# Regrouping attention heads by direct transfers between on-chip buffers, slot by slot

## The chip, the cores and the metric

The kernel runs on one core of one Trainium2 chip. The metric is device time in microseconds. A core has TensorE (PE, matmuls), VectorE (DVE), ScalarE (ACT) and GpSimd (POOL), each with its own list of instructions run in order; SyncE (SP) issues most of the DMA transfers, also in order; sixteen DMA engines carry them. Engines meet through semaphores: an instruction waits until a counter has reached a number, and adds to a counter when it is done. A DMA adds 16.

## The reference

x has 4 x 1024 tokens of 256 numbers. The "attention" mixes heads within a token and never tokens with each other. Then come a layer norm, a mixture of experts (32 experts, 4 picked per token) with a shared expert, and another layer norm, all in float32:

```
Q, K, V = (x @ W.T).reshape(b, s, 16, 16)  for W in Wq, Wk, Wv
scores  = einsum('bshd,bstd->bsht', Q, K) / 4        # 16 x 16 for each token
out     = einsum('bsht,bstd->bshd', softmax(scores), V).reshape(b, s, 256)
x = layernorm(x + out @ Wfc.T)
x = layernorm(x + experts(x, top 4 of 32) + shared_expert(x))
```

## The kernel before

The 4096 tokens go in 8 chunks of 512. For each chunk TensorE projects Q, K and V (`project`, six parts of 128 rows each), with the 256 rows of a projection on 2 x 128 partitions and the 512 tokens along a row. ScalarE copies each part to the buffers `QT`, `KT`, `VT` (`evacuate`). A token's 16 x 16 scores need another layout: there the 512 tokens are cut into 8 slots of 64, partition 16 t + d holds dimension d of slot t, and a row holds 16 heads x 64 tokens. Then one matmul does a token from each slot at once; `Q2`, `K2` and `V2` have zeros wherever slots would mix. The same way back leads from `O_sb`, which has the outputs in the slot layout, to `OT`, which `out_project` reads.

The kernel before changes layout through memory. SP writes a tensor to `q_slots` and the like, one piece of 64 tokens (256 bytes) at a time, waits until it has landed, and reads it back in rows of 4 KB: `write_q`, `write_k`, `write_v`, `read_q`, `read_k`, `read_v` (lines 322 to 369). For O the write has 4 KB rows and the read 256-byte pieces: `write_o`, `read_o` (lines 371 to 381). Per chunk these are 2 + 2 transfers for Q, 2 + 8 for K, 4 + 4 for V and 1 + 2 for O.

There is one `Q2`, one `K2`, one `V2` and one `O_sb`: the next chunk's Q and K may be read in only when the last score matmul of the chunk before is done (`s_ready`), V only after its last weighing matmul (`o_ready`), and O is copied out by ScalarE in two halves (`copy_o`, `o_copied`) before it is written. `OT` exists twice.

All orders are written out by hand. TensorE's list mixes the projections of chunks ahead with scores, weighing and output projection of chunks behind (`score`, `weigh`, `out_project`, lines 1017 to 1046). VectorE does softmax, residual sums (`residual`, line 1447), variance and the routing of tokens to experts. GpSimd does one small step of the layer norm (line 575) and scatters the routed rows to memory, 16 scatters a chunk (line 582). SP's list runs from line 383 to line 502. When all 8 chunks are routed, the expert stage begins: SP loads rows of an expert, TensorE transposes and multiplies them, and the results are scattered, loaded and summed. The big expert weights lie in the memory that the attention buffers had, and are loaded when these are free (lines 482 to 502).

In rows and views one line can stand for many steps: line 1003 is the helper for all matmuls, 670 and 673 are the copies of Q, K and V, 682 that of O. `wgu_sb` holds Q2, K2, V2 and O_sb; `wd_sb` holds QT, KT, VT and OT; `sx` holds the normalised tokens.

Of the kernel before, what the change touches and what calls it, by code (L numbers as in the profile page):

```python
# [5 lines left out]
F32 = mybir.dt.float32  # L6
# [79 lines left out]
def build(nc, xT, x, wqkv, wfc, wr, rbias, wsgu, wsd, wgu, wd, out):  # L86
    xs = nc.dram_tensor("expert_rows", [XROWS, ROW], F32).ap()
    z = nc.dram_tensor("pick_rows", [TOPK * NTOK, DM], F32).ap()
    q_slots = nc.dram_tensor("q_slots", [CH, SLOT, DM, GRP], F32).ap()
    k_slots = nc.dram_tensor("k_slots", [CH, SLOT, DM, GRP], F32).ap()  # L90
    v_slots = nc.dram_tensor("v_slots", [CH, SLOT, DM, GRP], F32).ap()
    o_slots = nc.dram_tensor("o_slots", [CH, SLOT, DM, GRP], F32).ap()

    with ExitStack() as ctx:
# [164 lines left out]
        q_wr k_wr v_wr o_wr q_rd k_rd v_rd o_rd  # L259
# [18 lines left out]
        NSMALL = 5 * 16  # L278
        NCONST = 13
# [24 lines left out]
        def slot_rows(dram, n):  # L304
            return dram[n].rearrange("t r g -> r t g")

        @block.sync
        def _(sp):
# [23 lines left out]
            def write_k(n):
                write_slots(k_slots, KT, n, 4, S["k_wr"])

            def write_v(n):
                sp.wait_ge(S["evac"], 6 * n + 6)
                for hh in range(KC):
                    for t in range(2):
                        sp.dma_start(v_slots[n].rearrange("(c t) r g -> t r c g", t=2)[t, hh * P:(hh + 1) * P],
                                     VT[:, hh, t * 256:(t + 1) * 256].rearrange("p (c g) -> p c g", c=4))\  # L340
                            .then_inc(S["v_wr"], 16)

            def read_q(n):
                sp.wait_ge(S["q_wr"], 32 * (n + 1))
                if n:
                    sp.wait_ge(S["s_ready"], 2 * n)
                rows = q_slots[n].rearrange("t (d h) g -> (t d) (h g)", d=HD)
                for half in range(QB):
                    sp.dma_start(Q2[half * 64:(half + 1) * 64, half * 1024:(half + 1) * 1024],
                                 rows[half * 64:(half + 1) * 64, :]).then_inc(S["q_rd"], 16)  # L350

            def read_k(n, pairs):
                sp.wait_ge(S["k_wr"], 32 * (n + 1))
                if n:
                    sp.wait_ge(S["s_ready"], 2 * n)
                rows = k_slots[n].rearrange("t (d h) g -> (t d) (h g)", d=HD)
                for pair in pairs:
                    for t in range(2 * pair, 2 * pair + 2):
                        sp.dma_start(K2[t * HD:(t + 1) * HD, (t % KB) * 1024:(t % KB + 1) * 1024],  # L359
                                     rows[t * HD:(t + 1) * HD, :]).then_inc(S["k_rd"], 16)  # L360

            def read_v(n):
                sp.wait_ge(S["v_wr"], 64 * (n + 1))
                if n:
                    sp.wait_ge(S["o_ready"], 2 * n)
                rows = v_slots[n].rearrange("t (j d) g -> (t j) (d g)", d=HD)
                for c in range(KB):
                    sp.dma_start(V2[c * 32:(c + 1) * 32, c * 1024:(c + 1) * 1024],  # L368
                                 rows[c * 32:(c + 1) * 32, :]).then_inc(S["v_rd"], 16)
# [35 lines left out]
            write_q(2)
            read_k(1, range(0, 1))
            read_q(1)
            read_k(1, range(1, 2))
            write_k(2)
            read_k(1, range(2, 4))  # L410
            load_xT(4)
            write_v(2)
            read_v(1)
            write_o(0)
            write_q(3)
            read_o(0)
            read_q(2)
            read_k(2, range(0, 2))
            write_k(3)
            read_k(2, range(2, 4))  # L420
# [3 lines left out]
            read_v(2)
            write_o(1)
            write_q(4)
            read_k(3, range(0, 1))
            read_o(1)
            read_k(3, range(1, 2))
            read_q(3)  # L430
            read_k(3, range(2, 3))
            write_k(4)
            read_k(3, range(3, 4))
            read_v(3)
            write_o(2)
            read_o(2)
            load_x(3)
            read_k(4, range(0, 1))
            read_q(4)
            read_k(4, range(1, 2))  # L440
            write_v(4)
            read_k(4, range(2, 3))
# [3 lines left out]
            write_q(5)
            write_k(5)
            read_q(5)
            read_k(5, range(0, 1))
            read_v(4)  # L450
            write_o(3)
            read_k(5, range(1, 4))
            read_o(3)
# [3 lines left out]
            write_q(6)
            read_v(5)
            write_o(4)
            read_q(6)  # L460
# [1550 lines left out]
```

## Time and profile before

| | us |
|---|---|
| median of 3 runs (578.54 to 580.25) | 580.22 |
| the profiled execution as a whole | 585.22 |
| its span in the profile | 583.4 |

| stage of the span, us | TensorE busy | VectorE busy | DMA share | GB/s |
|---|---|---|---|---|
| 20 to 120 | 95.30 | 51.20 | 0.95 | 243 |
| 120 to 245 | 113.13 | 102.03 | 0.86 | 265 |
| 245 to 312 | 60.06 | 47.21 | 0.71 | 257 |

The first two stages are attention and routing, the third is the end of routing; from about 312 us on the experts run. The time from outside is longer than the span, and the profiled execution is longer than the median; sums are made within it. A row of a timeline gives start and length in microseconds, and in brackets for how long its engine stood idle before it and what ended that.

### The profile page before, as it was taken

Reading aid. Unit: us, or ns where it says so; the run is one execution under the profiler, and the core shown is the slowest. Engines: PE = TensorE matmul, PEld = TensorE weight load, DVE = VectorE, ACT = ScalarE, POOL = GpSimd, SP = SyncE. Lnnn points to the kernel's source line nnn. Section 1 sums busy time; section 2 is a strip of 40 time slices with the busy share of each in tenths; the row PEclk is TensorE's granted clock in tenths of the full one; section 3 lists DMA queues with packets and bytes.
Section 4 is the critical chain, followed back from the end, with each engine's and each line's share of the span. In section 5 each row is a group of like instructions: output and inputs, shape, how many; then the busy total and the mean of one; then the engine's idle time right before and its main releaser. Section 6 shows DMA issues by size and latency. Waiting matters only on the chain.

```text
span 583.4 us, 16223 instructions
## 1 busy us (share of the span) xinstructions
PE 532.9 (91%) x4604; PEld 402.9 (69%) x4605; DVE 353.0 (61%) x1207; ACT 296.2 (51%) x641; POOL 285.1 (49%) x293
## 2 busy tenths in 40 slices
PE   5989999997979999789888999999999999988994
PEld 2445667565647566556445999999988888877883
DVE  2032647897876899677943444444446666555865
ACT  1324463765646574423403566666655555545454
POOL 5000000664676767567770466666666655555400
PEclk9999999998989999899997999999999999999999
DMA  7998998997697999799623354555577777778398
GB/s 252 250 245 201 235 258 200 275 258 219 206 273 241 275 272 406 258 405 348 232 102 85 112 152 144 161 183 171 160 224 227 226 238 222 230 220 295 138 386 292
DMA packets 132219, 135.31 MB, mean 232 GB/s; under 512 B 77128, under 2 KB 115535, under 8 KB 131536
## 3 DMA queue, kind: packets, MB, share of 16 engines
q1 hardware_dynamic: 105984, 87.53, 52.6%
q0 software_dynamic: 12672, 34.10, 15.4%
q10 hardware_dynamic: 13520, 13.13, 7.5%
q8 instruction: 25, 0.41, 0.3%
q14 instruction: 18, 0.15, 0.1%
HBM read 74.79 MB, written 60.96 MB: 233 GB/s over the span
## 4 chain that ended last, share of the span: by engine, by line
PE 49%; DMA 18%; DVE 14%; SPq 6%; issue 6%; ACT 3%; DVEq 2%; ACTq 1%; POOL 1%; POOLq 0%
PE bank L1003 44%; DMA o_slots<-wgu_sb 5%; DMA prod<-expert_rows 5%; PE bank L1359 3%; DMA wd_sb<-o_slots 3%; DMA wgu_sb<-pick_rows 2%; SPq L368 1%; DVEq L299 1%; DMA pick_rows<-prod,ids 1%; ACT sx L972 1%; SPq L359 1%; DVE hsT L1527 1%; DMA wqkv_sb<-in_wqkv 1%; DVE hsT L1524 1%; SPq L522 1%
## 5 line engine op out<-in xcount | busy, mean ns | idle before, releaser
L616 POOL DMA_INDIRECT pick_rows<-prod,ids x134 | 139.2, 1039 | 101.8 <-ACT prod L929 75.8
L582 POOL DMA_INDIRECT expert_rows<-stage,pos x128 | 127.2, 994 | 58.9 <-issue 36.4
L1003 PE MATMUL bank<-prod 128*128 128x128 f32 x1088 | 134.8, 278 | 0.6 <-DVE prod L1845 0.6
L1003 PEld LDWEIGHTS bank<-prod 128*128 128x128 f32 x1088 | 129.0, 194 | 1.0 <-issue 0.9
L1003 PE MATMUL bank<-wd_sb,wqkv_sb 128*128 128x512 f32 x192 | 91.9, 615 | 6.3 <-DMA wqkv_sb<-in_wqkv 6.3
L1845 DVE COPY prod<-wgu_sb 128x512 f32 x136 | 54.0, 438 | 67.7 <-issue 59.3
L929 ACT ACTIVATE prod<-bank,kept 128x256 f32<-128x256 f32 x136 | 57.3, 470 | 31.3 <-PE bank L1003 27.7
L1003 PEld LDWEIGHTS bank<-wgu_sb 128*32 128x32 f32 x2048 | 58.8, 136 | 20.2 <-issue 17.0
L1003 PE MATMUL bank<-wgu_sb 128*32 128x64 f32 x2048 | 66.2, 296 | 4.6 <-DMA wgu_sb<-k_slots 3.7
L1003 PE MATMUL bank<-wd_sb,prod 128*128 x272 | 70.1, 380 | 0.4 <-DVE prod L1863 0.4
L1003 PEld LDWEIGHTS bank<-wd_sb,wqkv_sb 128*128 128x128 f32 x192 | 35.2, 195 | 42.5 <-issue 36.1
L575 POOL TENSOR_TENSOR rstdt<-vepst,neg_half 128x4 f32<-128x4 f32 x8 | 9.2, 1155 | 102.7 <-DVE vepst L1460 102.6
L1359 PE MATMUL bank<-ident,prod 128*128 128x128 f32 x272 | 43.0, 282 | 11.4 <-DMA prod<-expert_rows 7.8
L1359 PEld LDWEIGHTS bank<-ident,prod 128*128 128x128 f32 x272 | 32.5, 143 | 25.7 <-issue 10.6
L1003 PEld LDWEIGHTS bank<-wd_sb,prod 128*128 128x128 f32 x272 | 46.5, 191 | 4.3 <-issue 0.8
L1863 DVE TENSOR_TENSOR prod<-prod,bank 128x256 f32<-128x256 f32 x68 | 28.6, 420 | 34.3 <-ACT prod L945 33.5
L1003 PE MATMUL bank<-prod,wsgu_sb 128*128 128x512 f32 x96 | 45.2, 619 | 3.9 <-DVE hsT L1527 3.9
L1003 PE MATMUL bank<-wfc_sb,wd_sb 128*128 128x256 f32 x128 | 35.1, 423 | 11.5 <-DMA wd_sb<-o_slots 10.8
L920 ACT ACTIVATE prod<-bank 128x512 f32<-128x512 f32 x68 | 40.6, 597 | 1.5 <-PE bank L1359 1.5
L1003 PEld LDWEIGHTS bank<-wfc_sb,wd_sb 128*128 128x128 f32 x128 | 26.2, 211 | 21.8 <-issue 17.1
L661 ACT ACTIVATE stage<-sx 128x1024 f32<-128x1024 f32 x32 | 33.9, 1059 | 12.4 <-DVE idw L1612 5.5
L945 ACT ACTIVATE prod<-bank 128x256 f32<-128x256 f32 x68 | 26.0, 382 | 27.2 <-PE bank L1003 24.4
(170 smaller groups left out, 650.9 us busy)
## 6 DMA issues: line engine op xcount, KB each, us to landing
prod<-expert_rows SPq DMA_DIRECT2D x136, 132.0 KB
wsgu_sb<-pick_rows ACTq DMA_DIRECT2D x32, 256.0 KB, 3.8
wgu_sb<-pick_rows SPq DMA_DIRECT2D x12, 512.0 KB, 10.7
wgu_sb<-in_wgu SPq DMA_DIRECT2D x2, 2560.0 KB, 13.1
expert_rows<-pad_rows SPq DMA_DIRECT2D x4, 1056.0 KB, 19.1
wd_sb<-in_xT SPq DMA_DIRECT2D x8, 512.0 KB, 5.0
q_slots<-wd_sb SPq DMA_DIRECT2D x16, 256.0 KB
k_slots<-wd_sb SPq DMA_DIRECT2D x16, 256.0 KB, 4.2
```

Of the source, the lines that this page charges most:

```text
L299: return eng.value_load(tab[0:1, bass.ds(quad + SLOTS, 1)], min_val=0, max_val=NE ** (QUAD + 2) - 1)
L575: pool.tensor_tensor(rstdt[:, :], vepst[:, :], neg_half[:, :], ALU.pow).then_inc(S["rstd_ready"], 1)
L582: pool.indirect_dma_start(xs, bass.IndirectOffsetOnAxis(ap=pos[e % 2][:, i, k:k + 1], axis=0), stage[:, i, k, :], None, bounds_check=XROWS ...
L616: pool.indirect_dma_start(z, bass.IndirectOffsetOnAxis(ap=index[:, j:j + 1], axis=0), rows[:, j, :], None, bounds_check=TOPK * NTOK - 1, o ...
L661: act.activation(stage[:, i, :, 0:DM], x1_of(e)[:, i, :].unsqueeze(1).broadcast_to([P, TOPK, DM]), ACT.Copy)
L920: act.activation(xtT[par][:, :], banks[2][:, :], ACT.Copy).then_inc(S["cX_copied"], 1)
L929: act.activation(to[:, j, :], banks[6 + par][:, j * DM:(j + 1) * DM], ACT.Copy, scale=kept[par][:, j, 1:2]).then_inc(S["cy_copied"], 1)
L945: act.activation(cth[par][:, :], banks[par][:, 0:2 * P], ACT.Silu)\
L1003: return pe.matmul(dst, lhsT, rhs, start=(k == 0), stop=(k == n - 1))
L1359: last = pe.transpose(banks[2][:, c:c + P], xt[par][:, j, k * P:(k + 1) * P], ident[:, :])
L1845: last = dve.tensor_copy(ws[par][:, j, :], wgu_sb[:, bass.ds(found[j], KC * 2 * EI)])
L1863: dve.tensor_tensor(hT[par][:, :], cth[par][:, :], banks[par][:, 2 * P:4 * P], ALU.mult)\
```

## The change

The four tensors in memory go, and with them every write and read. In their place stand `regroup_q`, `regroup_k`, `regroup_v` and `regroup_o`: for each of the 8 slots one transfer of 64 KB from buffer to buffer, between 128 partitions x 2 x 64 numbers on one side and 16 partitions x 16 x 64 on the other. So that the order of numbers agrees on both sides, the columns of the weights are permuted on the host. The transfers of a tensor count on one semaphore: `q_in`, `k_in`, `v_in`, `o_in`, 8 x 16 a chunk.

`QT`, `KT` and `VT` now exist twice: odd chunks use room in `sx` that the last three chunks' normalised tokens need later, and the last chunk's V uses a buffer of x. ScalarE therefore waits for the transfers of two chunks before when it copies, and for those of the last chunks in `normalise`. TensorE's instructions and their order are unchanged, only the semaphores they wait for. SP's list is written anew.

```
+        def qT_of(n):
+            return over(sx, (CH - 1) * TPC * DM, KC, CT) if n % 2 else QT
...
-            def write_slots(dram, tensor, n, done, landed):
-                sp.wait_ge(S["evac"], 6 * n + done)
-                for hh in range(KC):
-                    sp.dma_start(slot_rows(dram, n)[hh * P:(hh + 1) * P],
-                                 tensor[:, hh, :].rearrange("p (t g) -> p t g", t=SLOT))\
-                        .then_inc(landed, 16)
...
+            def regroup_q(n):
+                sp.wait_ge(S["evac"], 6 * n + 2)
+                if n:
+                    sp.wait_ge(S["s_ready"], 2 * n)
+                for t in range(SLOT):
+                    sp.dma_start(Q2[t * HD:(t + 1) * HD, (t // 4) * 1024:(t // 4 + 1) * 1024],
+                                 qT_of(n)[:, :, slot(t)]).then_inc(S["q_in"], 16)
...
+            def regroup_o(n):
                 sp.wait_ge(S["o_copied"], 2 * (n + 1))
...
+                for t in range(SLOT):
+                    sp.dma_start(OT[n % 2][:, :, slot(t)], O_sb[t * NH:(t + 1) * NH, :]).then_inc(S["o_in"], 16)
...
+            regroup_o(1)
+            regroup_v(2)
...
-                if a and j % 2 == 0:
-                    act.wait_ge(S[("q_wr", "k_wr", "v_wr")[j // 2]], (64 if j == 4 else 32) * a)
+                if a >= 2 and j % 2 == 0:
+                    act.wait_ge(S[("q_in", "k_in", "v_in")[j // 2]], IN * (a - 1))
...
                 if p:
-                    act.wait_ge(S["o_wr"], 16 * p)
+                    act.wait_ge(S["o_in"], IN * p)
...
+                if b >= CH - 3:
+                    act.wait_ge(S[("v_in", "k_in", "q_in")[b - (CH - 3)]], IN * (CH - 2 if b == CH - 3 else CH))
...
-                pe.wait_ge(S["q_rd"], 32 * (p + 1))
-                pe.wait_ge(S["k_rd"], 128 * (p + 1))
+                pe.wait_ge(S["q_in"], IN * (p + 1))
+                pe.wait_ge(S["k_in"], IN * (p + 1))
```

On SP, around the V of chunk 2, the kernel before has this piece of its list (L339 writes V, L368 reads it, L373 writes O, L318 loads x):

```order
L339 DMA v_slots<-wd_sb 128x4x64 [waits evac]
L339 DMA v_slots<-wd_sb 128x4x64 x3
L318 DMA prod<-in_x 128x4x256 [waits res_ready]
L368 DMA wgu_sb<-v_slots 32x1024 [waits o_ready,v_wr]
L368 DMA wgu_sb<-v_slots 32x1024 x3
L373 DMA o_slots<-wgu_sb 128x1024 [waits o_copied]
```

The kernel after has there the following (L335 is Q, L343 K, L359 O, L351 V, L317 the load of the transposed x):

```order
L335 DMA wgu_sb<-wd_sb 16x16x64 [waits s_ready,evac]
L335 DMA wgu_sb<-wd_sb 16x16x64 x7
L343 DMA wgu_sb<-wd_sb 16x16x64 [waits s_ready,evac]
L343 DMA wgu_sb<-wd_sb 16x16x64 x7
L317 DMA wd_sb<-in_xT 128x1024 [waits proj_ready]
L359 DMA wd_sb<-wgu_sb 128x2x64 [waits o_copied]
L359 DMA wd_sb<-wgu_sb 128x2x64 x7
L351 DMA wgu_sb<-wd_sb 16x16x64 [waits o_ready,evac]
L351 DMA wgu_sb<-wd_sb 16x16x64 x7
```

The O of chunk 1 stood behind the V of chunk 2 and now stands ahead of it.

On SP, from the Q of chunk 5 to the O of chunk 3, the kernel before has (L349 and L359 read Q and K, L373 and L380 write and read O):

```order
L349 DMA wgu_sb<-q_slots 64x1024 [waits s_ready,q_wr]
L349 DMA wgu_sb<-q_slots 64x1024
L359 DMA wgu_sb<-k_slots 16x1024 [waits s_ready,k_wr]
L359 DMA wgu_sb<-k_slots 16x1024
L368 DMA wgu_sb<-v_slots 32x1024 [waits o_ready,v_wr]
L368 DMA wgu_sb<-v_slots 32x1024 x3
L373 DMA o_slots<-wgu_sb 128x1024 [waits o_copied]
L359 DMA wgu_sb<-k_slots 16x1024 [waits s_ready,k_wr]
L359 DMA wgu_sb<-k_slots 16x1024 x5
L380 DMA wd_sb<-o_slots 128x8x64 [waits y_ready,o_wr]
L380 DMA wd_sb<-o_slots 128x8x64
```

and the kernel after (`sx` is the odd chunk's buffer):

```order
L335 DMA wgu_sb<-sx 16x16x64 [waits s_ready,evac]
L335 DMA wgu_sb<-sx 16x16x64 x7
L343 DMA wgu_sb<-sx 16x16x64 [waits s_ready,evac]
L343 DMA wgu_sb<-sx 16x16x64 x7
L359 DMA wd_sb<-wgu_sb 128x2x64 [waits y_ready,o_copied]
L359 DMA wd_sb<-wgu_sb 128x2x64 x7
```

All of K now goes ahead of O, and V of chunk 4, which stood between Q and O, has moved behind O.

## Rows read from the trace of the kernel before

**Rows 1.** The page's first line.

```profile
span 583.4 us, 16223 instructions
```

**Rows 2.** List of waits, TensorE for regrouping: total us, times, longest.

```profile
PE bank L1003 <- DMA wd_sb<-o_slots: 10.8, 5, 4.0
...
PE bank L1003 <- DMA wgu_sb<-k_slots: 3.7, 2, 2.6
```

**Rows 3.** TensorE's timeline: scores, weighing (wgu_sb) and output projection (wfc_sb).

```profile
35.64 2.21 PE L1003 MATMUL bank<-wgu_sb 128*32 128x64 f32 x64 [2.62 <-DMA wgu_sb<-k_slots]
...
65.44 1.97 PE L1003 MATMUL bank<-wfc_sb,wd_sb 128*128 128x256 f32 x8 [0.76 <-DMA wd_sb<-o_slots]
...
86.99 1.98 PE L1003 MATMUL bank<-wgu_sb 128*32 128x64 f32 x64
...
135.67 2.21 PE L1003 MATMUL bank<-wgu_sb 128*32 128x64 f32 x64 [1.07 <-DMA wgu_sb<-k_slots]
139.81 3.15 PE L1003 MATMUL bank<-wfc_sb,wd_sb 128*128 128x256 f32 x8 [1.94 <-DMA wd_sb<-o_slots]
...
167.69 3.65 PE L1003 MATMUL bank<-wfc_sb,wd_sb 128*128 128x256 f32 x8 [3.96 <-DMA wd_sb<-o_slots]
...
182.81 2.21 PE L1003 MATMUL bank<-wgu_sb 128*32 128x64 f32 x64
...
243.45 3.34 PE L1003 MATMUL bank<-wfc_sb,wd_sb 128*128 128x256 f32 x8 [3.40 <-DMA wd_sb<-o_slots]
```

**Rows 4.** Busy us by engine, granted clock, DMA share, GB/s, output matmuls at 167.69.

```profile
core 0: us, PE busy (x) PEld busy (x) DVE busy (x) ACT busy (x) POOL busy (x), PEclk, DMA share, GB/s
...
167.69:171.34 3.65, 3.65 (x9) 2.96 (x10) 0.91 (x5) 0.00 (x0) 2.74 (x4) 0.53 0.86 248
```

**Rows 5.** VectorE's timeline: its waits for TensorE.

```profile
143.10 0.70 DVE L1447 TENSOR_TENSOR prod<-prod,bank 128x512 f32<-128x512 f32 x1 [2.89 <-PE bank L1003]
...
171.48 0.69 DVE L1447 TENSOR_TENSOR prod<-prod,bank 128x512 f32<-128x512 f32 x1 [2.77 <-PE bank L1003]
...
185.09 0.69 DVE L1478 TENSOR_REDUCE smax<-bank 128x32 f32<-128x512 f32 x1 [3.69 <-PE bank L1003]
...
246.93 0.69 DVE L1447 TENSOR_TENSOR prod<-prod,bank 128x512 f32<-128x512 f32 x1 [0.70 <-PE bank L1003]
...
252.09 0.69 DVE L1447 TENSOR_TENSOR prod<-prod,bank 128x512 f32<-128x512 f32 x1 [1.99 <-PE bank L1003]
```

**Rows 6.** Two stretches: only 256-byte pieces in flight; the early stage.

```profile
30.20:31.20 1.00, 1.00 (x4) 0.43 (x3) 0.00 (x0) 0.03 (x1) 0.00 (x0) 1.00 1.26 285
...
20.00:120.00 100.00, 95.30 (x1202) 60.26 (x1204) 51.20 (x140) 48.48 (x84) 13.22 (x13) 1.00 0.95 243
```

**Rows 7.** Line 325, 12 to 40 us: ns to issue (min/median/max), landing.

```profile
L325 SPq DMA_DIRECT2D q_slots<-wd_sb x6: 386/508/584, 12.9 to 39.2; - x6
L325 SPq DMA_DIRECT2D k_slots<-wd_sb x4: 360/502/584, 16.5 to 31.5; - x4
...
DMA to landing us min/median/max: 2.3/2.7/3.1
```

**Rows 8.** SP's timeline: start, us for the transfers merged into one row.

```profile
12.89 1.01 SPq L325 DMA_DIRECT2D q_slots<-wd_sb  x2
...
46.31 4.27 SPq L359 DMA_DIRECT2D wgu_sb<-k_slots  x4
...
123.37 1.09 SPq L349 DMA_DIRECT2D wgu_sb<-q_slots  x2
...
195.97 3.59 SPq L359 DMA_DIRECT2D wgu_sb<-k_slots  x8
```

**Rows 9.** ScalarE's timeline: second halves of O copied, chunks 1, 4 and 7.

```profile
77.23 0.99 ACT L682 ACTIVATE wgu_sb<-bank 128x512 f32<-128x512 f32 x1
...
155.05 1.03 ACT L682 ACTIVATE wgu_sb<-bank 128x512 f32<-128x512 f32 x1
...
231.53 1.04 ACT L682 ACTIVATE wgu_sb<-bank 128x512 f32<-128x512 f32 x1
```

**Rows 10.** Line 349, reads of Q from memory: landing.

```profile
DMA to landing us min/median/max: 3.5/4.4/7.1
```

**Rows 11.** GpSimd's timeline: the layer norm step of chunk 7.

```profile
254.66 1.04 POOL L575 TENSOR_TENSOR rstdt<-vepst,neg_half 128x4 f32<-128x4 f32 x1 [2.68 <-DVE vepst L1460]
```

More of the change, by code:

```diff
@@ L173, in x1_of, with kT_of, vT_of @@
             return over(sx, b * TPC * DM, TPC, DM)
+        def qT_of(n):
+            return over(sx, (CH - 1) * TPC * DM, KC, CT) if n % 2 else QT
+        def kT_of(n):
+            return over(sx, (CH - 2) * TPC * DM, KC, CT) if n % 2 else KT
+        def vT_of(n):
+            if n == CH - 1:
+                return xT_sb[0]
+            return over(sx, (CH - 3) * TPC * DM, KC, CT) if n % 2 else VT
         stage = sb("stage", [P, TPC, TOPK, ROW])
@@ L332, in write_k @@
[L332 to L341, printed above, removed]
@@ L343, in read_q, with slot @@
-            def read_q(n):
-                sp.wait_ge(S["q_wr"], 32 * (n + 1))
+            def slot(n):
+                return slice(n * GRP, (n + 1) * GRP)
+            def regroup_q(n):
+                sp.wait_ge(S["evac"], 6 * n + 2)
                 if n:
                     sp.wait_ge(S["s_ready"], 2 * n)
[L347 to L350, printed above, removed]
@@ L352, in read_k, with regroup_k @@
-            def read_k(n, pairs):
-                sp.wait_ge(S["k_wr"], 32 * (n + 1))
+                for t in range(SLOT):
+                    sp.dma_start(Q2[t * HD:(t + 1) * HD, (t // 4) * 1024:(t // 4 + 1) * 1024],
+                                 qT_of(n)[:, :, slot(t)]).then_inc(S["q_in"], 16)
+            def regroup_k(n):
+                sp.wait_ge(S["evac"], 6 * n + 4)
                 if n:
                     sp.wait_ge(S["s_ready"], 2 * n)
[L356 to L360, printed above, removed]
@@ L362, in read_v, with regroup_v @@
-            def read_v(n):
-                sp.wait_ge(S["v_wr"], 64 * (n + 1))
+                for t in range(SLOT):
+                    sp.dma_start(K2[t * HD:(t + 1) * HD, (t % KB) * 1024:(t % KB + 1) * 1024],
+                                 kT_of(n)[:, :, slot(t)]).then_inc(S["k_in"], 16)
+            def regroup_v(n):
+                sp.wait_ge(S["evac"], 6 * n + 6)
                 if n:
                     sp.wait_ge(S["o_ready"], 2 * n)
[L366 to L369, printed above, removed]
@@ L371, in write_o @@
-            def write_o(n):
+                for t in range(SLOT):
+                    sp.dma_start(V2[t * NH:(t + 1) * NH, (t // 2) * 1024:(t // 2 + 1) * 1024],
+                                 vT_of(n)[:, :, slot((t % 2) * 4 + t // 2)]).then_inc(S["v_in"], 16)
+            def regroup_o(n):
                 sp.wait_ge(S["o_copied"], 2 * (n + 1))
-                sp.dma_start(o_slots[n].rearrange("t (h d) g -> (t h) (d g)", d=HD), O_sb).then_inc(S["o_wr"], 16)
-            def read_o(n):
-                sp.wait_ge(S["o_wr"], 16 * (n + 1))
@@ L405, in _ @@
[L405 to L410, printed above, removed]
-            load_xT(4)
[L412 to L420, printed above, removed]
+            load_xT(3)
+            regroup_q(1)
+            regroup_k(1)
@@ L421, in _ @@
+            regroup_o(0)
+            regroup_v(1)
+            load_xT(4)
+            regroup_q(2)
+            regroup_k(2)
             load_xT(5)
-            write_v(3)
+            regroup_o(1)
+            regroup_v(2)
             load_x(2)
[L424 to L436, printed above, removed]
-            load_x(3)
[L438 to L442, printed above, removed]
+            regroup_q(3)
+            regroup_k(3)
+            regroup_o(2)
+            load_x(3)
+            regroup_v(3)
+            regroup_q(4)
+            regroup_k(4)
             load_xT(6)
-            read_k(4, range(3, 4))
@@ L445, in _ @@
             load_x(4)
[L446 to L453, printed above, removed]
+            regroup_q(5)
+            regroup_k(5)
+            regroup_o(3)
+            regroup_v(4)
             load_xT(7)
-            write_v(5)
             load_x(5)
[L457 to L460, printed above, removed]
@@ L485, in _ @@
             sp.dma_start(wgu_sb[:, 0:width], wgu[:, 0:width]).then_inc(S["big_w"], 16)
-            write_o(7)
-            read_o(7)
+            for landed in ("q_in", "k_in", "v_in"):
+                sp.wait_ge(S[landed], IN * CH)
+            sp.dma_start(wd_sb[:, 0:WD_EARLY * DM], wd[:, 0:WD_EARLY * DM]).then_inc(S["big_w"], 16)
+            regroup_o(7)
             sp.wait_ge(S["o_ready"], 2 * CH)
-            sp.wait_ge(S["o_rd"], 32 * CH)
+            sp.wait_ge(S["o_in"], IN * CH)
             half = (GU_EARLY + 10) * KC * 2 * EI
```

80 lines of the change are left out of this document (29 added, 51 removed).

## The prediction

> **What bounds the kernel now.** I read the page first: one execution of 583.4 us span [rows 1]. Then, on the engine with the most work, the list of waits: all that TensorE waits for the regrouping of Q, K, V and O through memory is 10.8 us on O and 3.7 us on K [rows 2]. Then TensorE's timeline: in the attention stage (up to about 250 us) its instructions stand almost end to end, and the regrouping shows as gaps of 2.62 us at 35.64, 0.76 at 65.44, 1.07 at 135.67, 1.94 at 139.81, 3.96 at 167.69 and 3.40 at 243.45 [rows 3]. A gap costs more than its length: the eight output matmuls take 1.97 us at 65.44, but 3.15, 3.65 and 3.34 us behind the three long gaps [rows 3]; in the longest the granted clock was 0.53 of full [rows 4], nearly all at the lower level (1.2 GHz), after TensorE had stood idle. That is another 1.2, 1.7 and 1.4 us. In all 13.8 us of gaps and 4.3 of clock.
>
> But TensorE is not alone. VectorE's timeline from 113 us on is one run of work after another, each started by a wait for TensorE: 2.89 us before 143.10, 2.77 before 171.48, 3.69 before 185.09, 0.70 before 246.93, 1.99 before 252.09 [rows 5]. A lead that TensorE wins is passed on only until the gap on VectorE is closed. These gaps sum to 12.0 us. GpSimd, which writes the routed rows, waits 2.68 us at 254.66 for chunk 7's variance [rows 11] and from there works through; so the expert stage starts earlier by as much as that instruction does. Expert stage and tail hold none of the changed transfers: I leave them as they are.
>
> **The change part by part.** I call lead the time by which an instruction runs ahead of the kernel before.
>
> *DMA volume.* Each chunk's four tensors of 512 KB were written to memory and read back; now they move once. The 256-byte pieces remain, 2048 to a tensor. While such pieces alone were in flight they moved at 285 GB/s [rows 6], so 512 KB need 1.84 us of all engines. In the early stage the DMA engines were 0.95 busy at 243 GB/s [rows 6]; half the traffic of this kind goes. So DMA time is no longer the limit, if pieces from buffer to buffer cost what pieces to memory do (rival 1).
>
> *SP's issues.* 25 regrouping transfers a chunk become 32. The nearest shape, 128x8x64, is issued in 508 ns at the median, 360 at least [rows 7]; two of them stand in 1.01 us [rows 8]. With the gap to the next instruction I take p = 0.55 us, so 8p = 4.4 us for a tensor. Below, 0.40 (the 360 plus the gap); above, 1.07, the four K reads that took 4.27 us at 46.31, where SP was held back, as I read it, by a full queue [rows 8]. I take the value near the median, since the queue should be emptier: a tensor is issued in 4.4 us and moves in 1.84. A chunk now costs SP 32 x 0.55 plus two loads, 18.7 us, and TensorE's first five chunks follow each other at (135.67 - 35.64)/5 = 20.0 us [rows 3]. SP fits in, barely.
>
> *Tail.* From the last issue to landing I take 2.3 us, the least of the 256 KB stores while little else ran (median 2.7) [rows 7]; upper end 4.4, the median of the Q reads from memory [rows 10]; lower end 1.5, an estimate: 2.3 less the 0.9 that the 256 KB themselves need at 285 GB/s.
>
> *Chunk 0.* Q goes at 12.89 as before [rows 8], K behind it, landed 12.9 + 8.8 + 2.3 = 24.0; TensorE arrives at 35.64 - 2.62 = 33.0. Gap gone: lead 2.6. O(0) lands well before 62, so 0.76 goes too: lead 3.4.
>
> *A new wait: V(2).* SP runs in order, and O(1) now stands ahead of V(2). O(1) waits for its copy, which ended at 77.23 + 0.99 = 78.2 [rows 9], now 74.8; O(1) is issued to 79.2, V(2) to 83.6, landed 85.9. TensorE wants V(2) at 86.99 - 3.4 = 83.6 [rows 3]. Late by 2.3: lead 1.1. Behind it SP has next to no slack through chunks 3 and 4 (18.7 against 20.0).
>
> *Chunk 5 and O(3).* SP's issue of Q(5) started at 123.37 on the score before it [rows 8], now 122.2. Q(5) and K(5) are issued to 131.0, landed 133.3; TensorE is there at 135.67 - 1.07 - 1.1 = 133.5. The 1.07 goes: lead 2.2. O(3) follows, issued to 135.4, landed 137.7, against 139.81: lead 2.1, so most of that gap stays, as a wait behind two tensors of issues and no longer as a round trip. VectorE's start at 143.10 gains the same 2.1.
>
> *O(4).* Its copy ended at 155.05 + 1.03 [rows 9], now 154.0; issued to 158.4, landed 160.7. TensorE is there at 167.69 - 3.96 - 2.1 = 161.6. Gap and slow clock go. VectorE then has no gap before 171.48: lead 2.1 + 2.77 = 4.9. The score of chunk 6 stood 15.1 us behind these output matmuls (182.81 - 167.69), 13.4 without the slow clock: it starts at 175.0 and takes 2.21, so VectorE's start of 185.09 becomes 177.3: lead 7.8, which the rest up to O(7) keeps.
>
> *O(7).* Copied at 231.53 + 1.04 [rows 9], now 224.8; issued to 229.2, landed 231.5; the large weight loads ahead of it move by the same lead. TensorE wants it at 243.45 - 3.40 - 7.8 = 232.2. Gap and clock go; VectorE gains its 0.70 and 1.99: lead 10.5 at 252.09, and GpSimd's 254.66 follows, its work before being 7.8 ahead and its gap 2.68, just enough.
>
> *At nothing.* ScalarE's new waits before it overwrites Q, K and V buffers are for transfers two chunks back; those before the last three normalisations are for transfers that land tens of microseconds earlier by the above. Weights' columns are reordered on the host.
>
> Sum: 583.4 - 10.5 = 572.9 of span [rows 1]; the profiled execution as a whole took 585.22, so 574.7; it lies 5.0 above the median of the runs, 580.22, which becomes 569.7.
>
> **Rivals.**
>
> *1. Transfers into 16 partitions drain more slowly than they are issued.* For it: the 1.07 us apiece at 46.31 were such transfers [rows 8]. Against: eight of them went in 3.59 us at 195.97, 0.45 apiece [rows 8]. With p = 0.62 (the most in rows 7, 584 ns, with the gap) a tensor takes 5.0 us: Q(2), K(2) and V(2) come by the same walk 4.6 us late in all, K(4) 1.7, K(5) 1.0, so the lead at chunk 5 is about -3; then O(4), the score of chunk 6 and O(7) give their 8 back: lead 5, 575 us.
> The Trainium skill (SBUF — State Buffer, "Door 1: The DMA port swizzle") speaks for this: a transfer's rate depends on how many of 16 ports its partitions reach, and partitions 0 to 15 reach four, measured at 104 GB/s. By that rule 64 KB need about 0.63 us, an estimate from that figure; the row at 195.97 took in 64 KB each 0.45 us, 146 GB/s, which is above it, but shows acceptance and not landing. By the one the sum is 575, by the other 569.7.
>
> *2. The tail is as long as through memory.* With 4.4 us for 2.3, V(2) is late by 4.4, K(4) and K(5) by some 2, O(3) lands at 144.9; the late stages give back 7: lead 2, 578 us, hardly to be told from no change. For it: no landing among them is under 2.3 [rows 7, 10]. Against: those move 256 KB, these 64.
>
> *3. SP becomes the engine that bounds.* Nothing of this shape was ever issued here: a side of 128 partitions against one of 16. At p = 0.75 a chunk costs SP 25.1 us against the 20.0 of TensorE; four chunks lose 5.1 each, 20 us, and the 2.6 of the start and about 7 of the late gaps are all that returns: 591 us. It decides from p = (20.0 - 1.1)/32 = 0.59 on, and at 3.2 x 4 = 13 us per 0.1 us it eats the gain of 10.5 at about p = 0.67. For it: 1.07 in the full queue. Against: the median of 0.51 for a larger transfer of three dimensions.
>
> **How the numbers follow.** Forecast 0.50, its own range 563 to 574 (p from 0.40 to 0.60); rival 1 0.18; rival 2 0.12; rival 3 0.15; 0.05 for more than forecast (all 18 us of gap and clock, about 562). A measurement of this kernel can tell 0.3%, 1.7 us. Faster: forecast, rival 1, the small rest, and a quarter of rival 2, 0.75; same 0.10; slower 0.15. The range runs from 562 to 585, leaving out most of rival 3.
>
> **What would show it.** Right: SP's issues near 0.5 us, eight in 4 to 4.5 us; no gap on TensorE at the first score, none at O(4) and O(7), the output matmuls there back at 2 us; a new gap of about 2 us at the weighing of chunk 2, and some 2 us left at O(3); DMA share clearly under 0.9 in the first 120 us; the first expert transposes some 10 us earlier. Wrong: issues of 0.65 us or more, or gaps on TensorE for Q and K at chunks 2 to 5; then SP bounds. If the gaps go and the end does not come earlier, VectorE or GpSimd has taken them.

## The result and the profile after

The changed kernel takes 596.98 us (median of 4 runs, 594.18 to 598.8) against 580.24 us before (4 runs, 578.54 to 581.45): 1.0287 times as long, with a 95% interval of 1.0234 to 1.0339. The prediction was 569.7. The profiled execution of after was the fastest of its four, that of before (585.22) slower than all four of its runs, so the two traces differ by 9.0 us of span only [rows 1]; what is read from them are places, not the total.

The page of after: span, SP's DMA queue (packets, MB, share of 16 engines), the chain that ended last by engine.

```profile
span 592.4 us, 16265 instructions
...
q1 hardware_dynamic: 102784, 70.76, 41.5%
...
PE 47%; SPq 14%; DMA 13%; issue 9%; POOL 5%; ACT 4%; DVE 4%; DVEq 1%; ACTq 1%; POOLq 1%
```

The queue moves 16.8 MB less than before (87.53 MB); SP's share of the chain, SPq, is 14% where it was 6%.

TensorE's waits for the regrouping, against [rows 2] (total us, times, longest):

```profile
PE bank L937 <- DMA wgu_sb<-wd_sb: 10.6, 2, 5.7
...
PE bank L937 <- DMA wd_sb<-wgu_sb: 8.7, 3, 4.9
...
PE bank L937 <- DMA wgu_sb<-sx: 6.7, 3, 3.0
```

The waits for O (`wd_sb<-wgu_sb`) have fallen a little, from 10.8 to 8.7 us; those for Q and K (from `wd_sb` in even chunks, from `sx` in odd ones) have risen from 3.7 to 17.3. TensorE's timeline shows where, against [rows 3]:

```profile
32.95 2.21 PE L937 MATMUL bank<-wgu_sb 128*32 128x64 f32 x64
...
61.92 1.89 PE L937 MATMUL bank<-wfc_sb,wd_sb 128*128 128x256 f32 x8
...
77.95 2.21 PE L937 MATMUL bank<-wgu_sb 128*32 128x64 f32 x64 [4.99 <-DMA wgu_sb<-wd_sb]
...
102.13 2.21 PE L937 MATMUL bank<-wgu_sb 128*32 128x64 f32 x64 [1.50 <-DMA wgu_sb<-sx]
...
126.69 7.76 PE L937 MATMUL bank<-wgu_sb 128*32 128x64 f32 x256 [5.66 <-DMA wgu_sb<-wd_sb]
...
145.57 2.21 PE L937 MATMUL bank<-wgu_sb 128*32 128x64 f32 x64 [2.14 <-DMA wgu_sb<-sx]
152.67 3.63 PE L937 MATMUL bank<-wfc_sb,wd_sb 128*128 128x256 f32 x8 [4.89 <-DMA wd_sb<-wgu_sb]
...
180.07 3.58 PE L937 MATMUL bank<-wfc_sb,wd_sb 128*128 128x256 f32 x8 [3.01 <-DMA wd_sb<-wgu_sb]
...
220.52 2.21 PE L937 MATMUL bank<-wgu_sb 128*32 128x64 f32 x64 [3.03 <-DMA wgu_sb<-sx]
...
255.77 1.97 PE L937 MATMUL bank<-wfc_sb,wd_sb 128*128 128x256 f32 x8 [0.78 <-DMA wd_sb<-wgu_sb]
...
324.25 0.66 PE L1293 MATMUL bank<-ident,prod 128*128 128x128 f32 x4 [2.51 <-DMA prod<-expert_rows]
```

The last row is the first transpose of the expert stage. In the kernel before it stands at:

```profile
311.82 0.66 PE L1359 MATMUL bank<-ident,prod 128*128 128x128 f32 x4
```

The first scores start 2.7 us earlier (32.95 for 35.64). Then the scores of chunks 2, 3, 4 and 5 each wait, and the lead turns into a lag: 9.9 us at chunk 5 (145.57 for 135.67), 12.9 at O(3) (152.67 for 139.81). From there it stays: 12.4 at O(4), 12.3 at O(7), 12.4 at the first expert transpose (324.25 for 311.82). From there to the end of the span the kernel after takes 3.4 us less in these two executions, which makes the 9.0. The output matmuls behind the long gaps at O(3) and O(4) run at 3.6 us instead of 2. So the loss arises between 52 and 153 us. What does SP do there? Its timeline over one whole chunk of issues (L335 is Q, L343 K, L359 O, L351 V, L317 and L323 load x), against [rows 8]:

```profile
64.83 5.20 SPq L335 DMA_DIRECT2D wgu_sb<-wd_sb  x8
70.13 5.98 SPq L343 DMA_DIRECT2D wgu_sb<-wd_sb  x8
76.16 0.60 SPq L317 DMA_DIRECT2D wd_sb<-in_xT  x1
76.80 6.07 SPq L359 DMA_DIRECT2D wd_sb<-wgu_sb  x8
82.97 5.23 SPq L351 DMA_DIRECT2D wgu_sb<-wd_sb  x8
88.24 0.61 SPq L323 DMA_DIRECT2D prod<-in_x  x1
88.95 5.21 SPq L335 DMA_DIRECT2D wgu_sb<-sx  x8
```

Each row starts within 0.1 us of the end of the one above: SP issues almost without a pause, and one round (Q, K, O, V and two loads, 64.83 to 88.95) takes 24.1 us where TensorE took 20.0 a chunk before. The issue times of line 335 (ns, min/median/max), against [rows 7], and the early stage as a whole, against [rows 6]:

```profile
L335 SPq DMA_DIRECT2D wgu_sb<-wd_sb x32: 566/617/1488, 12.6 to 172.0; - x32
L335 SPq DMA_DIRECT2D wgu_sb<-sx x32: 565/618/1847, 39.3 to 211.4; - x32
```

```profile
20.00:120.00 100.00, 91.91 (x1108) 57.80 (x1107) 46.84 (x132) 44.71 (x76) 10.11 (x10) 0.97 0.53 130
```

An issue takes 0.617 us at the median and now and then 1.1 to 1.9 us; with the 0.04 to the next, eight take 5.2 us, and 5.7 to 6.5 when one of them is slow. The DMA engines meanwhile are busy to 0.53, at 130 GB/s, where they were at 0.95 and 243. The chain of waits from 60 to 130 us puts the two together:

```profile
by line: PE bank L937 28.2%; SPq L343 22.5%; SPq L335 19.9%; DMA wgu_sb<-wd_sb 7.1%; SPq L351 5.5%; issue 5.3%; DMA wgu_sb<-sx 3.3%; ACT sx L630 3.0%; ACT stage L593 1.3%; SPq L317 0.9%; ACT wd_sb L602 0.9%; PE bank L985 0.8%; ACT sx L602 0
...
75.49 2.32 DMA wgu_sb<-wd_sb
```

Nearly half of that stretch is SP issuing Q, K and V (22.5, 19.9 and 5.5%). The last issue of K(2) lands 2.32 us later, and TensorE starts.

### The profile page after: what moved, and what is told of

It reads as the page before. It is cut to its first block, busy times and chain, and to the rows that moved or that the text cites. A ratio compares the mean times of both kernels' runs of the same rounds, so it can differ in the third digit from the quotient of the medians.

```text
span 592.4 us, 16265 instructions
## 1 busy us (share of the span) xinstructions
PE 528.0 (89%) x4604; PEld 400.6 (68%) x4605; DVE 353.2 (60%) x1207; ACT 296.1 (50%) x641; POOL 286.4 (48%) x293
## 3 DMA queue, kind: packets, MB, share of 16 engines
q1 hardware_dynamic: 102784, 70.76, 41.5%
q0 software_dynamic: 12672, 34.10, 15.5%
## 4 chain that ended last, share of the span: by engine, by line
PE 47%; SPq 14%; DMA 13%; issue 9%; POOL 5%; ACT 4%; DVE 4%; DVEq 1%; ACTq 1%; POOLq 1%
PE bank L937 42%; SPq L335 4%; SPq L343 4%; PE bank L1293 4%; DMA pick_rows<-prod,ids 4%; DMA prod<-expert_rows 4%; POOL expert_rows L514 3%; SPq L359 3%; DMA wgu_sb<-pick_rows 2%; DMA wgu_sb<-sx 1%; SPq L351 1%; ACT sx L906 1%; DMA wd_sb<-wgu_sb 1%; SPq L449 1%; DMA wgu_sb<-wd_sb 1%
## 5 line engine op out<-in xcount | busy, mean ns | idle before, releaser
L937 PE MATMUL bank<-prod,wsgu_sb 128*128 128x512 f32 x96 | 43.5, 600 | 4.2 <-DVE hsT L1461 4.2
L1412 DVE TENSOR_REDUCE smax<-bank 128x32 f32<-128x512 f32 x16 | 10.9, 680 | 55.1 <-PE bank L937 55.0
L593 ACT ACTIVATE stage<-sx 128x1024 f32<-128x1024 f32 x32 | 34.3, 1076 | 12.4 <-DMA expert_rows<-stage,pos 7.5
L937 PEld LDWEIGHTS bank<-wfc_sb,wd_sb 128*128 128x128 f32 x128 | 25.9, 208 | 18.6 <-issue 12.9
## 6 DMA issues: line engine op xcount, KB each, us to landing
expert_rows<-pad_rows SPq DMA_DIRECT2D x4, 1056.0 KB, 19.9
```

Source lines behind the costliest of these rows:

```text
L593: act.activation(stage[:, i, :, 0:DM], x1_of(e)[:, i, :].unsqueeze(1).broadcast_to([P, TOPK, DM]), ACT.Copy)
L937: return pe.matmul(dst, lhsT, rhs, start=(k == 0), stop=(k == n - 1))
```

## Experiments

Theory S: SP's issue time per transfer, 0.66 us and more instead of the 0.55 of the prediction, makes SP the engine that bounds chunks 1 to 5. Theory D: the transfers drain slowly, at the side with 16 partitions or altogether. Theory O: SP's list has its entries in a bad order. Times of before in these comparisons are medians of 579.9 to 580.9 us.

### Half the bytes

```
-  sp.dma_start(Q2[.., c * 1024:(c + 1) * 1024],   qT_of(n)[:, :, t * 64:t * 64 + 64])
+  sp.dma_start(Q2[.., c * 1024:c * 1024 + 512],   qT_of(n)[:, :, t * 64:t * 64 + 32])    # K and V alike
```

> The changed kernel, but each Q, K and V transfer moves 32 of the 64 columns of its slot: as many transfers, half the bytes (the other half of the scores is computed from stale data). Theory S: an issue takes the same 0.6 us, SyncE stays end to end from 51 to 125 us, time 592 to 600 us. Theory D: the drain halves, time 575 us or less. If the issue time hangs on the bytes, it falls to 0.3 to 0.4 us and the time with it to 570 us or less, which would make S and D one thing.

Measured: 600.14 us, 1.0328 (1.0270 to 1.0386) of before. The issue times of Q in even chunks, and the early stage:

```profile
L338 SPq DMA_DIRECT2D wgu_sb<-wd_sb x32: 565/617/1668, 12.6 to 172.5; - x32
```

```profile
20.00:120.00 100.00, 92.19 (x1108) 57.95 (x1107) 46.77 (x131) 44.76 (x76) 9.83 (x10) 0.97 0.45 98
```

The same 617 ns for half the bytes, and about the same time: D falls as far as it hangs on bytes. The halved transfers consist of as many pieces, of 128 bytes instead of 256 (SP's queue has 103360 packets where the changed kernel's has 102784), so a drain that hangs on pieces is not excluded here; it is by Q through memory, below.

### Half the issues of Q and V

```
-  for t in range(SLOT):           # regroup_q and regroup_v
+  for t in range(0, SLOT, 2):
```

> The changed kernel, but Q and V move only every other slot (4 of 8 transfers each, left-out slots are not regrouped): 24 transfers a chunk for 32, three quarters of the bytes, everything on SyncE and in the same order. Theory S: SyncE needs 24 x 0.65 + 1.2 = 16.8 us a chunk against 20, time 563 to 575 us. Theory D: a quarter less to drain, the gaps shrink by a quarter, 588 to 594 us. Theory O (order): the same waits in the same order, so 590 us or more.

Measured: 574.92 us, 0.9899 (0.9863 to 0.9934). With 24 transfers a chunk in the same order the gaps at the scores of chunks 2 to 5 are gone, 22 us come back against the changed kernel. The scores are computed from stale data here, so other tokens may go to other experts; but the first expert transpose starts at 304.46 for 324.25, so 19.8 us of the gain arise ahead of the experts. Two longer waits are left, the longest at O(3):

```profile
85.43 1.98 PE L937 MATMUL bank<-wgu_sb 128*32 128x64 f32 x64 [2.06 <-issue]
...
139.63 3.65 PE L937 MATMUL bank<-wfc_sb,wd_sb 128*128 128x256 f32 x8 [4.56 <-DMA wd_sb<-wgu_sb]
```

O(3) waits behind the issues of Q(5) and K(5) even so: a matter of order, which is a smaller cause beside the number. The row at 85.43 is the weighing of chunk 2. The profile names no releaser for its wait, but the last transfer of V(2) is issued from 83.0, some 2.4 us before: it is the new wait that the prediction had put there, at 2.3.

### Order alone, early

```
-  regroup_o(1); regroup_v(2)        # and O(0), V(1); O(2), V(3)
+  regroup_v(2); regroup_o(1)
```

> The changed kernel with one difference, the order in SyncE's list: V(1), V(2) and V(3) stand ahead of O(0), O(1) and O(2) instead of behind them. Theory S: the number of issues a chunk is the same, SyncE stays end to end, 592 to 601 us, and only which instruction on TensorE waits changes. Theory O (the order is what costs, the wait for O(1)'s copy ahead of V(2), as the prediction had it): the early gaps shrink by some 2 us a chunk, 588 us or less.

Measured: 597.55 us, 1.0309 (1.0268 to 1.0350): as the changed kernel. The wait at the score of chunk 2 shrank (1.42 us for 4.99), that at the weighing of chunk 2 went (0.89 in the changed kernel), and the time came out elsewhere:

```profile
101.14 2.21 PE L937 MATMUL bank<-wgu_sb 128*32 128x64 f32 x64 [3.37 <-DMA wgu_sb<-sx]
113.43 3.75 PE L937 MATMUL bank<-wfc_sb,wd_sb 128*128 128x256 f32 x8 [5.31 <-DMA wd_sb<-wgu_sb]
```

While SP is full, order only chooses who waits.

### What an issue costs, by kind of transfer

Two kernels of nothing but transfers, run once each. All their issues stand under one helper line, so batches are told apart by names and time.

> A kernel that holds nothing but transfers, in batches with a wait for landing between them, and measures the issue time of each shape; the output is a copy of the input. Line 51: one 128x2x64 to 16x1024 alone; 54: 24 of these back to back; 57: 16x1024 to 128x2x64; 60: half the columns; 63: 16x1024 to 16x1024; 66: 16x1024 from memory; 69: 128x2x64 to the same shape; 72 and 75: 128x128 and 128x256; 78: 128x8x64 to memory in pairs; 82: 128x2x64 to rows in memory; 85: 128x64 alone; 88: 128x2x64 to 16x1024 one by one, each awaited; 97: the same from ScalarE. If the shape sets the issue time (a side of 128 partitions against one of 16), lines 54, 57, 82 and 88 stand near 0.6 us and the others at 0.4 to 0.5. If a full queue sets it, line 88 is well under line 54 and the first few of line 54 are short. If the number of dimensions sets it, 63, 66 and 72 stand near 0.4, 69 near 54.

In order: 128x2x64 to 16x1024 (one alone and 24 in a row), back from 16x1024, half the columns, 16x1024 to 16x1024, and 16x1024 out of memory; with the landing of the first batch:

```profile
L43 SPq DMA_DIRECT2D c<-a x25: 565/617/642, 22.2 to 40.0; - x25
...
DMA to landing us min/median/max: 2.6/2.8/2.9
...
L43 SPq DMA_DIRECT2D d<-b x8: 609/612/631, 42.6 to 47.2; - x8
...
L43 SPq DMA_DIRECT2D c<-a x8: 598/618/625, 49.8 to 54.5; - x8
...
L43 SPq DMA_DIRECT2D c<-b x8: 589/590/597, 56.5 to 61.0; - x8
...
L43 SPq DMA_DIRECT2D c<-rows x8: 338/420/421, 63.3 to 66.5; - x8
```

Neither unlike shapes nor a full queue explain the 0.62: 16x1024 to 16x1024 takes 0.59, the first one alone in an idle queue 0.642, and single ones, each awaited, 0.565 to 0.624. ScalarE's queue is no faster (0.612 to 0.642). All 24 in a row land 2.6 to 2.9 us after their issue, so nothing piles up: the drain keeps pace with 64 KB every 0.66 us, some 100 GB/s. The Trainium skill (SBUF — State Buffer, "Door 1: The DMA port swizzle") gives 104 GB/s for 16 partitions. At that rate 64 KB need 0.63 us, an estimate from that figure, so nothing would pile up here either; no run shows the limit itself.

> A second kernel of transfers alone, eight to a batch, to part the shape of a transfer from the kind of its two ends; the output is a copy of the input. In the first such kernel every transfer between buffers took 0.59 to 0.64 us to issue, also 128x128 to 128x128 (0.60) and also half the bytes, 16x1024 out of memory took 0.42, 128x512 into memory 0.39, but 128x2x64 into rows of memory 0.62. If each end in a buffer costs something, all batches with one end in memory stand at 0.3 to 0.45, however they are shaped, and the 0.62 stays unexplained. If an unlike shape of the two ends costs it, the batches of unlike shape (128x128 into 16 rows, 16 rows into 128x2x64) stand near 0.6 and those of like shape near 0.4, and transfers between buffers cost 0.6 for another reason. A large transfer between buffers (128x512) should cost no more than the small one, about 0.6.

128x2x64 into memory of the same shape; 128x128 into 16 rows of memory; 16 rows of memory into 128x2x64; 128x512 from buffer to buffer:

```profile
L46 SPq DMA_DIRECT2D pairs<-a x8: 613/620/622, 21.7 to 26.3; - x8
...
L46 SPq DMA_DIRECT2D rows<-b x8: 332/432/433, 28.3 to 31.6; - x8
...
L46 SPq DMA_DIRECT2D d<-rows x8: 592/612/612, 48.3 to 52.8; - x8
...
L46 SPq DMA_DIRECT2D c<-b x8: 465/559/603, 77.0 to 86.4; - x8
```

My guesses on shape fell in part. The picture: 0.42 to 0.43 us for two dimensions with one end in memory, alike or not; 0.56 to 0.60 for two dimensions from buffer to buffer, from 64 to 256 KB; 0.61 to 0.62 with a side of 128x2x64, wherever the other end is. The stores of 128x8x64 that I took my price from lie between, at 0.508 [rows 7]. What in a transfer makes the price these batches do not show.

### O from ScalarE's queue

```
+  def regroup_o(n):  ...  act.dma_start(OT[n % 2][:, :, slot], O_sb[..])   # after copy_o(n, 1)
-  regroup_o(0) ... regroup_o(7) in SP's list
```

> The changed kernel, with the eight O transfers of each chunk issued from ScalarE's queue instead of SyncE's; bytes, shapes and waits as they were. Theory S (SyncE's issue time, about 0.65 us apiece, is the bound in chunks 1 to 5): SyncE has 24 of them a chunk, 24 x 0.65 + 1.2 = 16.8 us against TensorE's 20, so the gaps ahead of the scores of chunks 2 to 5 (5.0, 1.5, 5.7, 2.1 us) fall under 1 us each, and the time is 565 to 577 us; ScalarE pays some 5 us a chunk, of which it has about half free. Theory D (transfers into 16 partitions drain slowly whoever issues them): the same bytes in the same shape, the gaps stay, 590 us or more. Theory O (SyncE waits in the wrong places: O stands ahead of V, and of the next Q and K): also faster, but SyncE's rows would still be end to end only where it waits; told apart by SyncE's timeline.

Measured: 609.22 us, 1.0525 (1.0452 to 1.0597), outside all that was expected. The gaps at the scores of chunks 2 and 3 went and that of chunk 4 fell from 5.66 to 1.80 us, as S has it; but later:

```profile
166.50 3.75 PE L938 MATMUL bank<-wd_sb,wqkv_sb 128*128 128x512 f32 x4 [5.50 <-ACT wd_sb L587]
...
242.17 3.75 PE L938 MATMUL bank<-wfc_sb,wd_sb 128*128 128x256 f32 x8 [13.55 <-DMA wd_sb<-wgu_sb]
```

```profile
157.60 6.29 ACTq L599 DMA_DIRECT2D wd_sb<-wgu_sb  x8
...
217.68 6.51 ACTq L599 DMA_DIRECT2D wd_sb<-wgu_sb  x8
```

```profile
221.89 0.61 SPq L401 DMA_DIRECT2D wgu_sb<-in_wgu  x1
224.65 0.35 SPq L404 DMA_DIRECT2D wd_sb<-in_wd  x1
```

ScalarE spends 6.3 us on eight issues and copies nothing meanwhile, and TensorE waits 5.50 us for its next copy. And O(6), issued from 217.68, now runs beside the two large weight loads, which SP's list had kept behind it: TensorE waits 13.55 us for it. The Trainium skill (DMA: Bandwidth & Descriptors, "Issuing engines are not separate DMA queues") says that a second issuing engine "will only save the time on the sequencer it takes to initiate the DMA, which is usually small relative to the DMA itself". The first half agrees with these rows: the time on SP was saved and no more, with the two queues in each other's way. The second does not hold here: an issue takes 0.62 us where 64 KB take some 0.23 us of the DMA engines (an estimate, by the 285 GB/s of [rows 6]), and 32 issues a chunk were the bound.

### O of chunks 0 to 2 alone from ScalarE's queue

> The changed kernel with O of chunks 0, 1 and 2 alone issued from ScalarE's queue; O(3) to O(7) stay on SyncE in their places ahead of the weight loads. Theory S: as with all O on ScalarE, the gaps for Q and K at chunks 2 to 4 go (TensorE then arrived at the scores of chunk 4 at 119.6 against 126.7); without the waits of 13.6 us at O(6) behind the weight loads and of 4 to 5.5 us for ScalarE in chunks 5 and 6, that lead of some 7 us over the changed kernel lasts: 584 to 590 us. If ScalarE's 5 to 6.5 us of issues per chunk cost as much as they free on SyncE: 594 us or more.

Measured: 588.42 us, 1.0117 (1.0074 to 1.0159): with the late O back ahead of the weight loads neither late wait is there, and 8.6 us of the changed kernel's time come back, as expected. Its edit is the one above for three chunks.

### Q through memory

```
-  regroup_q(n)                               # 8 transfers
+  write_q(n)  (2, right after the copies)  ...  read_q(n)  (2)
```

> The changed kernel, but Q alone goes through memory (two writes early, two reads instead of eight transfers). Theory S: SyncE needs 24 x 0.65 + 2 + 1.2 = 18.8 us a chunk against 20, so it fits in just: the gaps at the scores shrink to under 1.5 us each, 572 to 584 us. Theory D: more traffic than the changed kernel, 595 us or more.

Measured: 578.75 us, 0.9964 (0.9937 to 0.9990), in the range of S; no score waits more than 0.74 us. More bytes (74.95 MB on SP's queue for 70.76), no fewer packets (103296 for 102784), fewer issues, and 18 us faster than the changed kernel; D says the opposite, by bytes and by pieces.

### Q and the early O through memory

```
   regroup_k(2); write_q(3); load_xT(5)
-  regroup_o(1); regroup_v(2)
+  write_o(1); regroup_v(2); read_o(1)        # O(0) to O(3), O(3) around half of K(5)
```

> The changed kernel, but Q of every chunk, and O of chunks 0 to 3, go through memory again (Q: two writes early, two reads; O: one write, two reads, with V or K issues between write and read), K, V and the late O directly. Theory S: SyncE's issues a chunk are 16 x 0.65 for K and V, about 2 us for Q, 1.4 for O, 1.2 for the loads: 15 us against TensorE's 20. The gaps at the scores of chunks 2 to 5 and at O(3) go; what is left is O(4), about 1 us, and O(7): 567 to 575 us, better than both kernels. Theory D (the drain, or the DMA engines' traffic, is the bound): the traffic rises from the changed kernel's half to three quarters of before, so nothing is won: 590 us or more.

Measured: 578.31 us, 0.9976 (0.9944 to 1.0008), above what S allowed. The scores no longer wait; one place does for long:

```profile
106.59 3.75 PE L979 MATMUL bank<-wfc_sb,wd_sb 128*128 128x256 f32 x8 [5.34 <-DMA wd_sb<-o_slots]
```

I had put O(2)'s read behind a load that waits for VectorE, and behind V(3). Next, that alone was changed:

```
-  write_o(2); load_x(3); regroup_v(3); read_o(2)
+  write_o(2); read_o(2); load_x(3); regroup_v(3)
```

> The kernel with Q, and O of chunks 0 to 3, through memory, with one difference: O(2) is read back right behind its write, ahead of the load of x and V(3). In the kernel it comes from, SyncE issued the write at 92.47, waited, sent V(3) and read O(2) only at 102.42, so that TensorE waited 5.34 us for it and then ran 3.75 us at the lower clock for 1.97. Theory S, with the order in SyncE's list as the second cause: that gap falls under 1 us and about 6 us of lead come back at the score of chunk 4, of which VectorE's own waits pass on some 4 to 6: 571 to 575 us. If only the number of issues counts and order does not, no change: 578 us.

Measured: 572.28 us (6 runs, 568.83 to 573.88), 0.9843 (0.9809 to 0.9877): better than both kernels. Its early stage, and O(7), the gap there against 3.40 before:

```profile
20.00:120.00 100.00, 98.64 (x1325) 63.95 (x1327) 54.63 (x163) 51.29 (x87) 15.97 (x16) 1.00 0.79 199
```

```profile
230.63 3.75 PE L979 MATMUL bank<-wfc_sb,wd_sb 128*128 128x256 f32 x8 [0.86 <-DMA wd_sb<-wgu_sb]
```

TensorE is busy 98.6 of 100 us, with the DMA engines at 0.79: neither they nor SP, which issues nothing from 68.1 to 74.6 us for one, are at their end. Once SP has room, order counts: 6 us for one line. The output matmuls of O(7) take 3.75 us for 1.97, at a granted clock of 0.50 (the lower level): shortly before, up to 229.01, TensorE had stood idle for 3.43 us, waiting for ScalarE and not for a transfer.

### The late O alone, in the kernel before

```
-  write_o(n) ... read_o(n)          # n = 4 to 7; Wfc's columns reordered to fit
+  regroup_o(n)
```

> The kernel before with one part of the change: O of chunks 4 to 7 goes directly between buffers (eight transfers each), all else through memory as it was (Wfc's columns are reordered to fit). SyncE has about 15.5 us of issues a chunk there against 24 and more from score to score. Theory S: where SyncE has room the direct transfer does what the prediction's late steps said: the gap of 3.96 us at O(4) and that of 3.40 at O(7) fall under 1.5 us, the output matmuls there go back to 2 us, lead at the end 5 to 8 us, 572 to 576 us. Theory D (direct transfers land no sooner than two trips through memory): gaps as before, 580 us.

Measured: 576.66 us, 0.9922 (0.9892 to 0.9951), just above the range. The two places of [rows 3] in this kernel, and ahead of them O(3), which goes through memory in both kernels:

```profile
138.32 1.97 PE L1011 MATMUL bank<-wfc_sb,wd_sb 128*128 128x256 f32 x8 [0.37 <-DMA wd_sb<-o_slots]
...
163.12 1.97 PE L1011 MATMUL bank<-wfc_sb,wd_sb 128*128 128x256 f32 x8 [2.09 <-DMA wd_sb<-wgu_sb]
...
237.03 1.97 PE L1011 MATMUL bank<-wfc_sb,wd_sb 128*128 128x256 f32 x8 [0.36 <-DMA wd_sb<-wgu_sb]
```

3.96 became 2.09 and 3.40 became 0.36, both matmuls are back at 1.97 us, and O(7) runs 6.4 us earlier. Not all of that comes from the change: O(3), whose way is the same, waits 0.37 us here instead of 1.94 and runs at 1.97 us instead of 3.15, which makes 2.7 us between these two executions. The direct O gives the other 3.7, and the medians differ by 3.8 (580.49 before). O(4) still waits more than the 1.5 I had allowed: SP took 7.37 us for its eight issues there.

### Order alone, late

```
-  regroup_q(6); regroup_o(4)
+  regroup_o(4); regroup_q(6)
```

> The changed kernel with one difference in SyncE's list: O(4) stands ahead of Q(6) instead of behind it. In the changed kernel O(4)'s copy ended at 169.4, SyncE sent Q(6) from 166.54 to 172.65 and O(4) only from 172.75 to 178.11, and TensorE waited 3.01 us for it at 180.07 and then ran the output matmuls in 3.58 us instead of 1.97. Theory S with order as the second cause late on: O(4) goes at 169.5 and lands by 177.5, the gap and the slow clock go, 4.6 us of lead at that place, of which VectorE's waits (2.18 and 3.78 us behind it) let 2 to 4 through: 592 to 595 us. Rival: what the late stages have is again limited by the sum of issues (O(5), V(6), Q(7), K(7), O(6), V(7) are sent end to end from 194 to 231 us), so the lead is lost again at the score of chunk 7: 596 to 598 us.

Measured: 594.75 us (6 runs, 593.36 to 595.09), 1.0254 (1.0215 to 1.0293), which overlaps with the changed kernel's interval; 2.2 us by the medians.

```profile
176.47 1.97 PE L937 MATMUL bank<-wfc_sb,wd_sb 128*128 128x256 f32 x8 [0.17 <-DMA wd_sb<-wgu_sb]
```

The gap at O(4) is gone (0.17 for 3.01), but of the 3.6 us that O(4) is earlier (0.9 of them already at O(3), 151.79 for 152.67) 1.5 remain at the score of chunk 6 (193.66 for 195.12): ahead of the weighing of chunk 5, at 186.70, TensorE now stands idle for 3.10 us, with no releaser named, 2.7 us behind the start of V(5)'s last issue (184.0). A small gain is likely; the runs don't tell it apart from none.

## Why the prediction was wrong

The step that failed is SP's issues: "I take p = 0.55 us". Measured were 0.617 at the median and 0.66 with the gap; over the two rounds from 64.83 to 112.73 us, 64 transfers and 3 loads of some 0.65 took 47.9 us, so 0.72 apiece with the slow ones. The mechanism was in the prediction, as its rival 3, with the point from which it decides (0.59) and the price (4 us a chunk at 0.72); TensorE's lag grew by 4.3 us a chunk from the scores of chunk 1 to those of chunk 4 (116.47 before, 126.69 after, from a lead of 2.6). At the median alone, 0.66, rival 3 would have eaten just about the gain (its turning point is about 0.67); at 0.72 it makes a loss. What I got wrong was the chance: the nearest row was a store to memory, where the new transfers stay between buffers, and "SP fits in, barely" had 1.3 us a chunk to spare on a price that no row showed. A price with an upper bound of 1.07 and a turning point at 0.59 did not allow 0.15 for that rival.

Point by point:

- *DMA volume*: right. Half the traffic of this kind went, the share fell from 0.95 to 0.53. It gave nothing, since SP was the next limit.
- *Tail*: right. 2.3 to 2.6 us in the chain of waits, 2.6 to 2.9 in the kernel of transfers alone; rival 2 (4.4) falls. Rival 1, a slow drain, falls: in the transfers alone nothing piles up, half the bytes change nothing, and Q through memory, with more bytes and no fewer packets, is faster.
- *Chunk 0*: right, 2.7 for 2.6, and 3.5 for 3.4 at O(0) (61.92 for 65.44).
- *V(2)*: right in itself, and hidden here. TensorE already waited 4.99 us for Q(2) and K(2), which 0.55 had on time, and only 0.89 was left at the weighing (89.97). With half the issues of Q and V the wait is there, 2.06 for 2.3. While SP is full, V ahead of O gains nothing.
- *Chunk 5 and O(3)*: the mechanism, a wait behind two tensors of issues, was right; the size was not (4.89 us, at a lag of 12.9 instead of a lead of 2.1).
- *O(4)*: wrong in itself. The step sends O(4) as soon as it is copied, but Q(6) stood ahead of it in SP's list, 6.1 us of issues that I had not counted. With the two exchanged the gap goes.
- *O(7)*: right in place (0.78 us left, matmuls at 1.97), but a wait of 3.03 us at the score of chunk 7 took what it gave: there, too, SP was full, and rival 3's "about 7 of the late gaps" did not come back.
- *Rival 3's sum*: by its formula 0.72 costs 4.1 us a chunk, 16.6 in four; measured are 15.5, from a lead of 2.6 at the scores of chunk 1 to a lag of 12.9 at O(3). With nothing back behind that, the lag stays near 12.4. That the medians lie 16.7 apart, and not 12.4, the two traces do not show.
- *VectorE and GpSimd*: they took none of the lag: GpSimd's step of [rows 11] runs at 267.16 for 254.66, 12.5 us later.
- *At nothing*: ScalarE's waits before it overwrites V cost it 4.0 us once, a consequence of SP's lag.

That the late steps hold where SP has room is shown in part by the kernel before with the late O alone direct: gaps and slow clock at O(4) and O(7) shrink or go, but of the 6.4 us of lead at O(7) 3.7 are the direct O's, where the prediction's late part had 8.3 (10.5 less 2.2).

## What to carry to other kernels

Count the issues per round of each queue and multiply by the price of exactly that kind of transfer: fewer bytes in more transfers can be slower, and here a buffer-to-buffer transfer was not issued at the price of a store. Where the price isn't in the trace, measure it in a kernel of transfers alone, before the rewrite. And mix: the slower path with fewer issues where the queue is full, the direct one where its latency is waited for, gave 572.28 us.

## What the hardware showed

- SP's issue time hung on the kind of a transfer and not on its bytes: 0.42 to 0.43 us for 64 KB in two dimensions with one end in memory, 0.56 to 0.60 between buffers (64 to 256 KB), 0.61 to 0.62 with a side of 128x2x64.
- In the changed kernel an issue took 1.1 to 1.9 us now and then, about one in a batch of eight or none; in the kernel of transfers alone those of 64 KB and less never took more than 0.71 us. What makes them slow stays open.
- The loads of a whole 512 KB chunk of x took 0.60 us at the median behind such transfers (line 317, 8 loads, 389 ns the least), 0.42 in the kernel before; this was not followed up.
